# Experts' stage of a two-layer attention and expert network: loops written out, transposes one expert ahead, weights in two parts, finer waits at the tail

## The chip, the cores and the metric

One Trainium2 chip, one of its cores. The metric is the device time of one execution in microseconds; lower is better. The core has five engines that run side by side and meet at semaphores: TensorE (PE in the profile; PEld is its weight load), VectorE (DVE), ScalarE (ACT), GpSimd (POOL) and SyncE (SP), which issues most of the DMAs.

## What is computed

The whole reference is two layers, each an attention and a feed-forward part. The change touches only the last part, a mixture of experts over 2048 tokens of width 256:

```python
xt = x.reshape(T, d)                                    # T = 2048, d = 256
probs = softmax(xt @ Wg); eidx = argmax(probs); gate = probs[eidx]
pos = rank of the token among those of its expert
keep = pos < C                                          # C = 256, E = 8 experts
xd = rows of xt put at eidx * C + pos                   # (8, 256, 256)
h = silu(xd @ W1[e]) * (xd @ W3[e]); oe = h @ W2[e]     # hidden width 352
out = oe[eidx * C + pos] * gate * keep
shared = silu(xt @ sw1) * (xt @ sw3) @ sw2
x = x + out + shared
```

## The kernel before

`phase_moe` cuts its work into 16 pieces of 256 tokens. Eight are pieces of the shared network (0 to 7) and eight are the experts' own (0 to 7). TensorE runs them in this order: shared 0 to 5 (`HEAD` is 6), experts 0 to 7, shared 6 and 7 (`TAILS`). A piece has two parts. `hidden` (L2323) multiplies by the two upper weights, in three column blocks f = 0, 1, 2 (128, 128 and 96 wide), each block in its own PSUM bank `psH[f]`; every float32 matmul of the code is two instructions, so a block is 8 and a piece's `hidden` is 24. For every block ScalarE makes silu (`silu`, L2405), VectorE multiplies (`gated`, L2441, tile `g`). `down` (L2333) multiplies `g` by the lower weights, 12 instructions, into `psY[0]` and `psY[1]`; VectorE then adds the result to `x` (`add_shared`, L2449) or scales it by the gate into `yo` (`weigh`, L2457), and GpSimd scatters `yo` to `routed_scr` in DRAM with two indirect DMAs per expert (L2307).

In a shared piece TensorE runs block 0 of the piece, then `down` of the piece before, then blocks 1 and 2. In an expert's piece (`own`) the order is: four transposes of the expert's rows `xd[:, e]` into `psH[3]` (L2363), `down` of the piece before, then all three blocks. ScalarE copies the transposed rows to `xt` (L2410, in its `own`) before the expert's silus.

The rows of an expert come about so: logits and ranks are made on TensorE and VectorE while shared 0 and 1 run. Then GpSimd scatters the 16 row tiles with one indirect DMA each (L2300) to `xd_scr`, and SP, after waiting for all of them, loads `xd` for each expert (L2264).

On TensorE, ScalarE and VectorE shared pieces 2 to 5 (on ScalarE 0 to 5) are a hardware loop (`Fori`), on ScalarE the experts too, on SP the weight loads of experts 2 to 7. The double-buffered weights are loaded by four DMAs (`load_ffn`, L2231 to L2234) on one semaphore, when `down` of the expert two before is done (`y_full`). At the end SP waits for the last scatter, loads `back` from `routed_scr` in quarters (L2276), VectorE adds the quarters to `x` (L2528), the first three after the last `gated` and the fourth after the last `add_shared`, and SP sends every quarter out (L2281).

Of the kernel before, what the change touches and what calls it, by code (L numbers as in the profile page):

```python
# [9 lines left out]
ALU = mybir.AluOpType  # L10
# [6 lines left out]
P = 128  # L17
# [6 lines left out]
NT = B * ST  # L24
# [2134 lines left out]
def phase_moe(nc, ctx, t, keep, x, rows, xT):  # L2159
# [4 lines left out]
    def sem(name):  # L2164
        return new_semaphore(nc, "m_" + name)
# [41 lines left out]

    in_c, in_s, in_z = sem("in_c"), sem("in_s"), sem("in_z")
    in_w = [sem(f"in_w{i}") for i in range(2)]
    in_xd = [sem(f"in_xd{e}") for e in range(E1)]  # L2210
    in_back = [sem(f"in_back{k}") for k in range(4)]
    emptied, named, gates_ready = sem("emptied"), sem("named"), sem("gates_ready")
# [14 lines left out]
    TAILS = [(HEAD + E1 + i, HEAD + i) for i in range(NS - HEAD)]  # L2227
    norm = Norm(nc, ctx, keep, x, xn, xT, "m_", psH)

    def load_ffn(sp, s, d1, d3, d2, a1, a3, a2):  # L2230
        sp.dma_start(d1[:], a1.rearrange("(c d) f -> d c f", d=P)).then_inc(s, 16)  # L2231
        sp.dma_start(d3[:], a3.rearrange("(c d) f -> d c f", d=P)).then_inc(s, 16)
        sp.dma_start(d2[:, 0:2, :], a2[0:256, :].rearrange("(c f) d -> f c d", f=P)).then_inc(s, 16)
        sp.dma_start(d2[0:96, 2, :], a2[256:352, :]).then_inc(s, 16)  # L2234

    with nc.Block() as block:
        @block.sync
        def _(sp):
            sp.dma_start(ident[:], t["ident"]).then_inc(in_c, 16)
            sp.dma_start(upper[:], t["upper"]).then_inc(in_c, 16)  # L2240
            sp.dma_start(rank[:], t["rank"]).then_inc(in_c, 16)
            sp.dma_start(ebase[:], t["ebase"]).then_inc(in_c, 16)
            sp.dma_start(token[:], t["token"]).then_inc(in_c, 16)
            sp.dma_start(wg[:], t["L1_ffn_Wg"].rearrange("(c d) e -> d c e", d=P)).then_inc(in_c, 16)
            load_ffn(sp, in_s, sw1, sw3, sw2, t["L1_ffn_sw1"], t["L1_ffn_sw3"], t["L1_ffn_sw2"])
            sp.wait_ge(emptied, 2)
            for k in range(4):
                sp.dma_start(t["xd_scr"].rearrange("(k p r) d -> k p (r d)", k=4, p=P)[k],
                             empty[:].rearrange("p r d -> p (r d)")).then_inc(in_z, 16)

            def weights(e, u):
                ap = [a[bass.ds(e, 1)].rearrange("o a b -> (o a) b")
                      for a in (t["L1_ffn_W1"], t["L1_ffn_W3"], t["L1_ffn_W2"])]
                load_ffn(sp, in_w[u], w1[u], w3[u], w2[u], *ap)

            weights(0, 0)
            weights(1, 1)
            sp.wait_ge(zeroed, 1)
            for k in range(4):
                sp.dma_start(t["routed_scr"].rearrange("(k p r) d -> k p (r d)", k=4, p=P)[k],  # L2260
                             zero[:]).then_inc(in_z, 16)
            sp.wait_ge(scattered, 16 * NT)
            for e in range(E1):
                sp.dma_start(xd[:, e], t["xd_scr"][e * CAP1:(e + 1) * CAP1, :].rearrange("(c p) d -> p c d", p=P)  # L2264
                             ).then_inc(in_xd[e], 16)
            with sp.Fori(0, E1 // 2 - 1) as j:
                for u in range(2):
                    e = 2 * j + u

                    sp.wait_ge(y_full, 2 * (HEAD + e) + 2)  # L2270
                    weights(e + 2, u)
            for u in range(2):
                sp.wait_ge(sent[u], 32 * (E1 // 2))
            for k in range(4):
                rows_k = slice(k * NT // 4, (k + 1) * NT // 4)
                sp.dma_start(back[:, rows_k, :],  # L2276
                             t["routed_scr"].rearrange("(j p) d -> p j d", p=P)[:, rows_k, :]).then_inc(in_back[k], 16)
            for k in range(4):
                rows_k = slice(k * NT // 4, (k + 1) * NT // 4)
                sp.wait_ge(x_final, k + 1)  # L2280
                sp.dma_start(t["out"].rearrange("b (s p) d -> p (b s) d", p=P)[:, rows_k, :],  # L2281
                             x[:, rows_k, :]).then_inc(out_sent, 16)
            for u in range(2):
                sp.wait_ge(in_w[u], 64 * (E1 // 2))
            sp.wait_ge(out_sent, 64)

        @block.gpsimd
        def _(pool):
# [25 lines left out]
        def _(pe):  # L2314
# [34 lines left out]
            def shared(n, i, last):  # L2349

                moving = (lambda c: xT[:, c, i * CAP1:(i + 1) * CAP1] if isinstance(i, int) else
                          xT[:, c, bass.ds(i * CAP1, CAP1)])
                hidden(n, sw1, sw3, moving, 0)
                if last is not None:
                    down(*last)
                hidden(n, sw1, sw3, moving, 1)

            def own(e, j, u, last):
                pe.wait_ge(in_xd[e], 16)
                pe.wait_ge(xt_done, e + 1)  # L2360
                for c in range(DK):
                    for r in range(2):
                        mm = pe.transpose(psH[3][:, c * 256 + r * P:c * 256 + (r + 1) * P],  # L2363
                                          xd[:, e, r, c * P:(c + 1) * P], ident[:])
                mm.then_inc(xt_full, 1)
                down(*last)
                pe.wait_ge(in_w[u], 64 * j + 64)
                pe.wait_ge(xt_done, e + 2)
                hidden(HEAD + e, w1[u], w3[u], lambda c: xt[u][:, c, :], 0)
                hidden(HEAD + e, w1[u], w3[u], lambda c: xt[u][:, c, :], 1)  # L2370

            shared(0, 0, None)
            shared(1, 1, (0, sw2, 0))
# [8 lines left out]
                               ohb[:, j:j + 1, :].broadcast_to([P, left, E1]),  # L2382
                               start=False, stop=True, skip_group_check=True)
            mm.then_inc(cum_full, 1)
            with pe.Fori(1, HEAD // 2) as j:
                for u in range(2):
                    n = 2 * j + u
                    shared(n, n, (n - 1, sw2, 1 - u))
            own(0, 0, 0, (HEAD - 1, sw2, 1))
            for e in range(1, E1):  # L2390
                own(e, e // 2, e % 2, (HEAD + e - 1, w2[(e - 1) % 2], (e - 1) % 2))
            last = (HEAD + E1 - 1, w2[1], 1)
            for n, i in TAILS:
                shared(n, i, last)
                last = (n, sw2, n % 2)
            down(*last)

        @block.scalar
        def _(act):
# [5 lines left out]
                    nc.scalar.activation(act_s[u][0:fw, f, :], psH[f][0:fw, 0:CAP1], ACT.Silu  # L2405
                                         ).then_inc(silu_done, 1)

            def own(e, u):
                act.wait_ge(xt_full, e + 1)
                nc.scalar.activation(xt[u][:].rearrange("p c s -> p (c s)"), psH[3][:],  # L2410
                                     ACT.Copy).then_inc(xt_done, 1)
                silu(HEAD + e, u)

            norm.scalar_root(act)
            norm.scalar_columns(act)
            act.wait_ge(l_done, 2)
            nc.scalar.activation(ex[:], ex[:], ACT.Exp).then_inc(ex_ready, 1)
            with act.Fori(0, HEAD // 2) as j:
                for u in range(2):
                    silu(2 * j + u, u)  # L2420
            act.sem_inc(xt_done, 1)
            with act.Fori(0, E1 // 2) as j:
                for u in range(2):
                    own(2 * j + u, u)
            for n, _ in TAILS:
                silu(n, n % 2)

# [1 line left out]
        def _(dve):  # L2429
# [14 lines left out]
            def add_shared(n, i):  # L2444

                for r in range(2):
                    dve.wait_ge(y_full, 2 * n + r + 1)
                    row = x[:, bass.ds(2 * i + r, 1), :].rearrange("p o d -> p (o d)")
                    nc.vector.tensor_tensor(row, row, psY[r][:, 0:D], ALU.add).then_inc(y_done, 1)  # L2449

            def weigh(e):

# [46 lines left out]
            link(nc.vector.tensor_scalar(keepm[:], keepm[:], -OUT_OF_RANGE, OUT_OF_RANGE, ALU.mult, ALU.add))  # L2499
            link(nc.vector.tensor_tensor(slot[:], slot[:], keepm[:], ALU.add))  # L2500
            nc.vector.tensor_copy(s_idx[:], slot[:]).then_inc(idx_ready, 1)
            with dve.Fori(1, HEAD // 2) as j:
                for u in range(2):
                    n = 2 * j + u
                    gated(n, u, (0,))
                    add_shared(n - 1, n - 1)
                    gated(n, u, (1, 2))
            add_shared(HEAD - 1, HEAD - 1)
            for e in range(E1):
                if e > 0:  # L2510
                    weigh(e - 1)
                gated(HEAD + e, e % 2)
            for k, (n, i) in enumerate(TAILS):
                gated(n, n % 2, (0,))
                if k == 0:
                    weigh(E1 - 1)
                else:
                    add_shared(n - 1, i - 1)
                gated(n, n % 2, (1, 2))

            dve.wait_ge(y_done, 2 * n + 2)
            for k in range(4):
                rows_k = slice(k * NT // 4, (k + 1) * NT // 4)
                if k == 3:
                    add_shared(n, i)
                    dve.wait_ge(y_done, 2 * n + 4)
                dve.wait_ge(in_back[k], 16)
                nc.vector.tensor_tensor(x[:, rows_k, :], x[:, rows_k, :], back[:, rows_k, :],  # L2528
                                        ALU.add).then_inc(x_final, 1)

# [164 lines left out]
```

## Time and profile before

| | us |
|---|---|
| median of 3 runs | 1718.06 (1713.58 to 1718.11) |
| the profiled execution's own time | 1718.32 |
| its span, first to last instruction | 1716.5 |
| mean granted TensorE clock | 0.97 |
| last stage's first instruction to the end of the span | 1534.6 to 1716.5 |

Engines' busy shares over the span are PE 95%, DVE 77%, ACT 59%, POOL 58%. The profile is of one execution, and times in the rows are microseconds from the start of its span. A row's bracket says how long the engine had been idle before and what released it.

### The profile page before, as it was taken

To read this page: it belongs to the slowest core of one execution; us is meant where nothing else is said; L and a number is where in the kernel's file an instruction comes from. 1 tells how busy PE (TensorE), PEld (TensorE's weight loads), DVE (VectorE), ACT (ScalarE), POOL (GpSimd) and SP (SyncE) were. 2 spreads that over 40 slices of the span, in tenths; PEclk is the share of its full clock that TensorE was granted. 3 is DMA by queue.
4 is the path that set the end of the run, shared out by engine and by line. 5 is a ranking of instruction groups with operands and counts; after the bars stand their busy time and mean duration, and the time that the engine had idled before them with its cause. 6 is when DMAs were issued, how large, how long until landed. Compare 5 with 4: busy or idle time off the path is not lost. (4 is left out here: it accounts for less than half of the span.)

```text
span 1716.5 us, 49117 instructions
## 1 busy us (share of the span) xinstructions
PE 1632.6 (95%) x16165; PEld 1311.5 (76%) x16165; DVE 1320.2 (77%) x3025; ACT 1018.0 (59%) x2039; POOL 991.8 (58%) x879
## 2 busy tenths in 40 slices
PE   5889999999999999999999999999999899969898
PEld 4678888888888888888888888887886455548676
DVE  6888888888888888888888888887884588873123
ACT  5876666666666666666666666665333466642111
POOL 5348777878878787778788787777000222211221
PEclk8599999999999999999999999999999999987999
DMA  9721121121121122122112116114820000013244
GB/s 254 245 69 44 52 72 47 46 79 43 41 82 42 43 71 58 39 62 63 47 54 70 43 47 152 41 49 121 178 58 1 13 14 13 12 64 133 84 156 141
DMA packets 183005, 126.16 MB, mean 73 GB/s; under 512 B 107434, under 2 KB 170200, under 8 KB 182576
## 3 DMA queue, kind: packets, MB, share of 16 engines
q1 hardware_dynamic: 181424, 121.60, 25.7%
q0 software_dynamic: 1536, 3.99, 0.6%
q8 instruction: 25, 0.41, 0.1%
q14 instruction: 20, 0.16, 0.0%
HBM read 82.04 MB, written 24.48 MB: 62 GB/s over the span
## 5 line engine op out<-in xcount | busy, mean ns | idle before, releaser
L1174 POOL TENSOR_TENSOR c_rest<-c_prob 128x1024 f16<-128x1024 f32 (+1 forms) x513 | 796.0, 1572 | 242.8 <-ACT c_prob L963 232.5
L963 ACT ACTIVATE c_prob<-c_psS,ln,c_exp_scale 128x1024 f32<-128x1024 f32 (+1 forms) x514 | 536.5, 1044 | 241.2 <-PE c_psS L799 236.0
L1068 DVE TENSOR_REDUCE c_mxp<-c_psM 128x1 f32<-128x400 f32 (+1 forms) x1040 | 588.4, 572 | 113.8 <-PE c_psM L783 97.0
L799 PE MATMUL c_psS<-c_q,c_kk 128*128 128x256 f16 (+1 forms) x3350 | 512.7, 272 | 0.2 <-issue 0.2
L817 PE MATMUL c_psV<-c_vb,c_prob 128*128 128x129 f16 (+1 forms) x3328 | 396.5, 222 | 0.7 <-ACT c_acc L1017 0.7
L799 PEld LDWEIGHTS c_psS<-c_q,c_kk 128*128 128x128 f16 (+1 forms) x3350 | 321.8, 99 | 85.7 <-issue 0.4
L820 PE MATMUL c_psV<-c_vb,c_rest 128*128 128x65 f16 (+1 forms) x3328 | 374.2, 193 | 0.0
L783 PE MATMUL c_psM<-c_kkm,c_q 128*128 128x400 f16 (+1 forms) x1040 | 346.1, 333 | 4.7 <-DVE c_mxp L1068 3.0
L820 PEld LDWEIGHTS c_psV<-c_vb,c_rest 128*128 128x128 f16 (+1 forms) x3328 | 301.4, 99 | 22.1
L817 PEld LDWEIGHTS c_psV<-c_vb,c_prob 128*128 128x128 bf16 (+1 forms) x3328 | 305.3, 97 | 15.3 <-ACT c_acc L1017 1.0
L745 PE MATMUL c_psQ<-c_xb,c_w2s 128*128 128x256 f16 x1188 | 164.1, 275 | 5.8 <-PEq L162 4.0
L2051 ACT ACTIVATE g_prob<-g_psS,g_bias 128x128 f32<-128x128 f32 (+1 forms) x264 | 106.6, 425 | 47.3 <-DVE g_bias L2092 47.3
L745 PEld LDWEIGHTS c_psQ<-c_xb,c_w2s 128*128 128x128 f16 x1188 | 102.8, 98 | 23.0 <-issue 6.9
L1844 POOL TENSOR_TENSOR km<-kT,g_hmask 128x1024 f32<-128x1024 f32 x18 | 34.1, 1915 | 136.3 <-PE g_psS L1957 136.3
L783 PEld LDWEIGHTS c_psM<-c_kkm,c_q 128*128 128x128 f16 x1040 | 101.7, 98 | 14.2 <-DVE c_mxp L1068 3.9
L770 PE MATMUL c_psQ<-c_roped,c_ms 128*128 128x256 f32 x396 | 101.5, 392 | 0.6 <-DVE c_roped L1052 0.6
L951 ACT ACTIVATE c_q<-c_psM 32x128 f16<-32x128 f16 x258 | 68.9, 267 | 49.2 <-PE c_psM L787 47.8
L2405 ACT ACTIVATE m_s<-m_psH 128x256 f32<-128x256 f32 (+1 forms) x48 | 18.3, 382 | 114.4 <-PE m_psH L2323 108.5
L939 ACT ACTIVATE c_q<-c_psQ 64x256 f16<-64x256 f32 x132 | 49.8, 378 | 50.3 <-PE c_psQ L770 48.7
L1239 POOL TENSOR_SCALAR xn_rows<-x_rows,f_n_agg,f_n_rstd 128x256 f32<-128x256 f32 x3 | 3.9, 1315 | 127.3 <-DVEq L1256 127.3
L2441 DVE TENSOR_TENSOR m_g<-m_s,m_psH 128x256 f32<-128x256 f32 (+1 forms) x48 | 20.2, 420 | 72.8 <-ACT m_s L2405 62.0
L770 PEld LDWEIGHTS c_psQ<-c_roped,c_ms 128*128 128x128 f32 x396 | 70.0, 190 | 7.6 <-DVE c_roped L1052 0.8
(301 smaller groups left out, 2266.0 us busy)
## 6 DMA issues: line engine op xcount, KB each, us to landing
c_w2s<-w_scr SPq DMA_DIRECT2D x66, 256.0 KB, 2.6
c_ms<-m_scr SPq DMA_DIRECT2D x67, 192.0 KB, 2.3
c_w2s<-w_scr SPq DMA_DIRECT2D x66, 128.0 KB, 2.0
acc_scr<-c_acc SPq DMA_DIRECT2D x129, 64.0 KB, 2.0
kv<-acc_scr SPq DMA_DIRECT2D x16, 512.0 KB, 6.6
m_w<-in_L_ffn_W SPq DMA_DIRECT2D x16, 352.0 KB, 4.2
c_vb<-V SPq DMA_DIRECT2D x27, 129.0 KB, 2.0
c_kk<-KK SPq DMA_DIRECT2D x27, 128.0 KB, 2.0
```

Source lines behind the costliest of these rows:

```text
L745: mm = pe.matmul(out, weights[:, w, c], xb[:, x, c, :], start=(c == 0 and i == 0), stop=(c == DK - 1 and i == 2))
L770: mm = pe.matmul(psQ[:, S:2 * S], ms[:, e, :], roped[:, e, :], start=(e == 0), stop=(e == 2))
L783: pe.matmul(psM[:, st, 0:w], q1[slot][:, st * P:(st + 1) * P], kkm[:, c0:c0 + w], start=True, stop=True).then_inc(mx_full, 1)
L799: mm = pe.matmul(psS[g % 2][0:r, i * S:(i + 1) * S], src[:, (lo + i) * P:(lo + i) * P + r], mov[slot][:, :], start=(one == 0 and i % 2 == ...
L817: pe.matmul(psV[:, st * W:(st + 1) * W], high[0:r, c0:c0 + P], vb[0:r, i, :], start=(i == 0 and st == 0), stop=False, skip_group_check=True)
L820: mm = pe.matmul(psV[:, st * W + DC:(st + 1) * W], rest[g][0:r, c0:c0 + P], vb[0:r, i, DC:W], start=False, stop=(i == LT - 1), skip_group_ ...
L939: nc.scalar.activation(q1[slot + u][rows, :], psQ[rows, S:2 * S], ACT.Copy).then_inc(qh_done, 1)
L951: last = nc.scalar.activation(q2[slot][0:2 * SHIFT_ROWS, st * P:(st + 1) * P], shiftT[st * 2 * SHIFT_ROWS:(st + 1) * 2 * SHIFT_ROWS, :], A ...
L963: nc.scalar.activation(prob[g][0:r, 0:w], psS[g % 2][0:r, 0:w], ACT.Exp, bias=keep["ln1024"][0:r, :], scale=exp_scale[slot][0:r, :]).then_ ...
L1068: nc.vector.tensor_reduce(mxp[:, st, c:c + 1], psM[:, st, 0:CHUNKS[c][1]], AX.X, ALU.max).then_inc(mx_done, 1)
L1174: nc.gpsimd.tensor_tensor(rest[g][0:r, 0:w], prob[g][0:r, 0:w], high[0:r, 0:w], ALU.subtract).then_inc(rest_done, 1)
L2051: ins = nc.scalar.activation(prob[k % 2][:, i * w:(i + 1) * w], psS[k % 2][:, i * w:(i + 1) * w], ACT.Exp, bias=bias[k % 2][:, i:i + 1], a ...
```

## The change

The loops of TensorE, ScalarE, VectorE and SP in this stage are written out. An expert's piece takes the order of a shared piece, block 0, `down` of the piece before, blocks 1 and 2, with the transposes of the next expert between `down` and block 1. The first expert's transposes stand in shared 5. The upper weights wait for `h_full` of the expert two before, the lower ones for its `y_full`, on semaphores of their own (`in_w`, `in_d`). At the tail, the last `down` runs block by block for both halves (`down_last`), the quarters of `back` are added earlier, and the last four row tiles leave in three DMAs.

```diff
+    in_d = [sem(f"in_d{i}") for i in range(2)]
...
-            with sp.Fori(0, E1 // 2 - 1) as j:
-                for u in range(2):
-                    e = 2 * j + u
-
-                    sp.wait_ge(y_full, 2 * (HEAD + e) + 2)
-                    weights(e + 2, u)
+            for e in range(2, E1):
+                sp.wait_ge(h_full, FTN * (HEAD + e - 2) + FTN)
+                up(e)
+                sp.wait_ge(y_full, 2 * (HEAD + e - 2) + 2)
+                lower(e)
...
-            for k in range(4):
-                rows_k = slice(k * NT // 4, (k + 1) * NT // 4)
-                sp.wait_ge(x_final, k + 1)
-                sp.dma_start(t["out"].rearrange("b (s p) d -> p (b s) d", p=P)[:, rows_k, :],
-                             x[:, rows_k, :]).then_inc(out_sent, 16)
+            for lo, hi in ((0, 4), (4, 8), (8, 12), (12, 14), (14, 15), (15, 16)):
+                sp.wait_ge(x_final, min(lo // 4 + 1, 4))
+                if lo >= NT - 2:
+                    sp.wait_ge(y_done, 2 * TAILS[-1][0] + 3 + lo - (NT - 2))
+                sp.dma_start(t["out"].rearrange("b (s p) d -> p (b s) d", p=P)[:, lo:hi, :],
+                             x[:, lo:hi, :]).then_inc(out_sent, 16)
...
                 hidden(n, sw1, sw3, moving, 0)
                 if last is not None:
+                    if n == HEAD + E1:
+                        pe.wait_ge(in_d[(E1 - 1) % 2], 32 * ((E1 - 1) // 2) + 32)
                     down(*last)
+                if n == HEAD - 1:
+                    transposes(0)
                 hidden(n, sw1, sw3, moving, 1)
...
-                down(*last)
-                pe.wait_ge(in_w[u], 64 * j + 64)
+
+            def own(e, last):
+                u = e % 2
+                pe.wait_ge(in_w[u], 32 * (e // 2) + 32)
                 pe.wait_ge(xt_done, e + 2)
                 hidden(HEAD + e, w1[u], w3[u], lambda c: xt[u][:, c, :], 0)
+                if e > 0:
+                    pe.wait_ge(in_d[1 - u], 32 * ((e - 1) // 2) + 32)
+                down(*last)
+                if e + 1 < E1:
+                    transposes(e + 1)
                 hidden(HEAD + e, w1[u], w3[u], lambda c: xt[u][:, c, :], 1)
+
+            def down_last(n, a2, u):
+                pe.wait_ge(y_done, 2 * n + 2)
+                for f, (_, fw) in enumerate(FT1):
+                    pe.wait_ge(g_done, FTN * n + 4 + f)
+                    for r in range(2):
+                        mm = pe.matmul(psY[r][:, 0:D], g[u][0:fw, f, r * P:(r + 1) * P], a2[0:fw, f, :],
+                                       start=(f == 0), stop=(f == FTN - 1))
+                        if f == FTN - 1:
+                            mm.then_inc(y_full, 1)
...
-            with pe.Fori(1, HEAD // 2) as j:
-                for u in range(2):
-                    n = 2 * j + u
-                    shared(n, n, (n - 1, sw2, 1 - u))
+            for n in range(2, HEAD):
+                shared(n, n, (n - 1, sw2, 1 - n % 2))
...
+            for n in range(HEAD + E1):
+                silu(n, n % 2, (0,))
+                if HEAD - 1 <= n < HEAD + E1 - 1:
+                    columns(n - HEAD + 1)
+                silu(n, n % 2, (1, 2))
...
+            def add_routed(k):
+                rows_k = slice(k * NT // 4, (k + 1) * NT // 4)
+                dve.wait_ge(in_back[k], 16)
+                nc.vector.tensor_tensor(x[:, rows_k, :], x[:, rows_k, :], back[:, rows_k, :],
+                                        ALU.add).then_inc(x_final, 1)
...
-                gated(n, n % 2, (1, 2))
-
-            dve.wait_ge(y_done, 2 * n + 2)
-            for k in range(4):
-                rows_k = slice(k * NT // 4, (k + 1) * NT // 4)
-                if k == 3:
-                    add_shared(n, i)
-                    dve.wait_ge(y_done, 2 * n + 4)
-                dve.wait_ge(in_back[k], 16)
-                nc.vector.tensor_tensor(x[:, rows_k, :], x[:, rows_k, :], back[:, rows_k, :],
-                                        ALU.add).then_inc(x_final, 1)
+                    dve.wait_ge(y_done, 2 * n + 2)
+                for f in (1, 2):
+                    if k == 1:
+                        add_routed(f - 1)
+                    gated(n, n % 2, (f,))
+            add_routed(2)
+            add_routed(3)
+            dve.wait_ge(x_final, 4)
+            add_shared(n, i)
```

## Rows read from the trace of the kernel before

**Rows 1.** The chain that ended last: start us, us, what.

```profile
1588.10 2.60 PE m_psY L2333 x12
1590.69 5.18 PE m_psH L2323 x24
1595.88 6.90 issue
1602.78 5.15 PE m_psY L2333 x12
```

**Rows 2.** Timeline, 1590 to 1604: start us, us, engine, line, op.

```profile
1590.53 5.34 PE L2323 MATMUL m_psH<-xT_rows,m_sw 128*128 x24
1596.85 0.38 ACT L2405 ACTIVATE m_s<-m_psH 128x256 f32<-128x256 f32 x1 [8.33 <-PE m_psH L2323]
1601.81 0.38 ACT L2405 ACTIVATE m_s<-m_psH 96x256 f32<-96x256 f32 x1 [4.58 <-remote]
...
1603.57 4.22 SPq L2264 DMA_DIRECT2D m_xd<-xd_scr  x8
```

**Rows 3.** The scatter's line L2300: durations ns min/median/max, first and last start.

```profile
L2300 POOL DMA_INDIRECT xd_scr<-xn_rows,m_s_idx x16: 972/972/1307, 1581.8 to 1601.3; - x16
```

**Rows 4.** A stretch: us, busy PE PEld DVE ACT POOL, PEclk, DMA share, GB/s.

```profile
1603.00:1619.00 16.00, 16.00 (x64) 13.07 (x64) 3.78 (x9) 2.40 (x6) 0.00 (x0) 0.86 0.44 133
```

**Rows 5.** Timeline of one expert's piece, 1631 to 1646.

```profile
1631.76 5.34 PE L2323 MATMUL m_psH<-m_xt,m_w 128*128 128x256 f32 x24
...
1636.94 0.60 PE L2363 MATMUL m_psH<-m_ident,m_xd 128*128 128x128 f32 x4
...
1637.55 0.42 DVE L2441 TENSOR_TENSOR m_g<-m_s,m_psH 96x256 f32<-96x256 f32 x1 [1.30 <-ACT m_s L2405]
...
1638.02 2.86 PE L2333 MATMUL m_psY<-m_w,m_g 128*128 128x256 f32 x12 [0.48 <-DVE m_g L2441]
...
1640.72 5.34 PE L2323 MATMUL m_psH<-m_xt,m_w 128*128 128x256 f32 x24
```

**Rows 6.** Timeline of the tail, 1702 to 1716.

```profile
1702.84 3.62 PE L2323 MATMUL m_psH<-xT_rows,m_sw 128*128 128x256 f32 x16
1703.04 0.42 DVE L2449 TENSOR_TENSOR x_rows<-x_rows,m_psY 128x256 f32<-128x256 f32 x1 [0.88 <-PE m_psY L2333]
...
1705.18 0.42 DVE L2441 TENSOR_TENSOR m_g<-m_s,m_psH 128x256 f32<-128x256 f32 x1 [1.72 <-ACT m_s L2405]
...
1706.90 0.42 DVE L2441 TENSOR_TENSOR m_g<-m_s,m_psH 96x256 f32<-96x256 f32 x1 [1.30 <-ACT m_s L2405]
1707.24 3.48 DVE L2528 TENSOR_TENSOR x_rows<-x_rows,m_back 128x1024 f32<-128x1024 f32 x3
...
1707.38 2.86 PE L2333 MATMUL m_psY<-m_sw,m_g 128*128 128x256 f32 x12 [0.92 <-DVE m_g L2441]
1708.48 4.57 SPq L2281 DMA_DIRECT2D out_dram<-x_rows  x4
1710.65 0.74 DVE L2449 TENSOR_TENSOR x_rows<-x_rows,m_psY 128x256 f32<-128x256 f32 x2
1711.42 1.23 DVE L2528 TENSOR_TENSOR x_rows<-x_rows,m_back 128x1024 f32<-128x1024 f32 x1
```

**Rows 7.** The loads of the experts' rows, L2264.

```profile
DMA to landing us min/median/max: 2.7/5.1/5.8
```

**Rows 8.** The loads of the experts' results, L2276, issued from 1699.0 to 1700.6.

```profile
DMA to landing us min/median/max: 3.8/5.4/6.8
```

**Rows 9.** The stores of the output, L2281.

```profile
DMA to landing us min/median/max: 3.0/3.4/3.8
```

**Rows 10.** The first of an expert's four weight DMAs, L2231.

```profile
DMA to landing us min/median/max: 3.2/3.4/6.5
```

**Rows 11.** TensorE's loop branches, lines L893 (attention of layer 0) and L2385.

```profile
L893 PEldq COMPARE_BRANCH  x32: 76/208/252, 140.8 to 1188.5; - x32
...
L2385 PEldq COMPARE_BRANCH  x2: 76/146/217, 1590.2 to 1615.2; - x2
```

More of the change, by code:

```diff
@@ L2228, in phase_moe, with load_up, load_down @@
     norm = Norm(nc, ctx, keep, x, xn, xT, "m_", psH)
-    def load_ffn(sp, s, d1, d3, d2, a1, a3, a2):
+    def load_up(sp, s, d1, d3, a1, a3):
         sp.dma_start(d1[:], a1.rearrange("(c d) f -> d c f", d=P)).then_inc(s, 16)
         sp.dma_start(d3[:], a3.rearrange("(c d) f -> d c f", d=P)).then_inc(s, 16)
+    def load_down(sp, s, d2, a2):
         sp.dma_start(d2[:, 0:2, :], a2[0:256, :].rearrange("(c f) d -> f c d", f=P)).then_inc(s, 16)
@@ L2244, in _ @@
             sp.dma_start(wg[:], t["L1_ffn_Wg"].rearrange("(c d) e -> d c e", d=P)).then_inc(in_c, 16)
-            load_ffn(sp, in_s, sw1, sw3, sw2, t["L1_ffn_sw1"], t["L1_ffn_sw3"], t["L1_ffn_sw2"])
+            load_up(sp, in_s, sw1, sw3, t["L1_ffn_sw1"], t["L1_ffn_sw3"])
+            load_down(sp, in_s, sw2, t["L1_ffn_sw2"])
             sp.wait_ge(emptied, 2)
@@ L2249, in _, with up, lower @@
                              empty[:].rearrange("p r d -> p (r d)")).then_inc(in_z, 16)
[L2251 to L2257, printed above, removed]
+            def up(e):
+                load_up(sp, in_w[e % 2], w1[e % 2], w3[e % 2], t["L1_ffn_W1"][e], t["L1_ffn_W3"][e])
+            def lower(e):
+                load_down(sp, in_d[e % 2], w2[e % 2], t["L1_ffn_W2"][e])
+            for e in range(2):
+                up(e)
+                lower(e)
             sp.wait_ge(zeroed, 1)
@@ L2265, in _ @@
                              ).then_inc(in_xd[e], 16)
-            with sp.Fori(0, E1 // 2 - 1) as j:
-                for u in range(2):
-                    e = 2 * j + u
-                    sp.wait_ge(y_full, 2 * (HEAD + e) + 2)
-                    weights(e + 2, u)
+            for e in range(2, E1):
+                sp.wait_ge(h_full, FTN * (HEAD + e - 2) + FTN)
+                up(e)
+                sp.wait_ge(y_full, 2 * (HEAD + e - 2) + 2)
+                lower(e)
             for u in range(2):
@@ L2277, in _ @@
                              t["routed_scr"].rearrange("(j p) d -> p j d", p=P)[:, rows_k, :]).then_inc(in_back[k], 16)
-            for k in range(4):
-                rows_k = slice(k * NT // 4, (k + 1) * NT // 4)
-                sp.wait_ge(x_final, k + 1)
-                sp.dma_start(t["out"].rearrange("b (s p) d -> p (b s) d", p=P)[:, rows_k, :],
-                             x[:, rows_k, :]).then_inc(out_sent, 16)
+            for lo, hi in ((0, 4), (4, 8), (8, 12), (12, 14), (14, 15), (15, 16)):
[4 more added lines that the diff above has]
+                             x[:, lo:hi, :]).then_inc(out_sent, 16)
             for u in range(2):
-                sp.wait_ge(in_w[u], 64 * (E1 // 2))
-            sp.wait_ge(out_sent, 64)
+                sp.wait_ge(in_w[u], 32 * (E1 // 2))
+                sp.wait_ge(in_d[u], 32 * (E1 // 2))
+            sp.wait_ge(out_sent, 96)
         @block.gpsimd
@@ L2354, in shared, with transposes @@
                 if last is not None:
+                    if n == HEAD + E1:
+                        pe.wait_ge(in_d[(E1 - 1) % 2], 32 * ((E1 - 1) // 2) + 32)
                     down(*last)
+                if n == HEAD - 1:
+                    transposes(0)
                 hidden(n, sw1, sw3, moving, 1)
-            def own(e, j, u, last):
+            def transposes(e):
                 pe.wait_ge(in_xd[e], 16)
@@ L2384, in _ @@
             mm.then_inc(cum_full, 1)
-            with pe.Fori(1, HEAD // 2) as j:
-                for u in range(2):
-                    n = 2 * j + u
-                    shared(n, n, (n - 1, sw2, 1 - u))
-            own(0, 0, 0, (HEAD - 1, sw2, 1))
+            for n in range(2, HEAD):
+                shared(n, n, (n - 1, sw2, 1 - n % 2))
+            own(0, (HEAD - 1, sw2, 1))
             for e in range(1, E1):
-                own(e, e // 2, e % 2, (HEAD + e - 1, w2[(e - 1) % 2], (e - 1) % 2))
+                own(e, (HEAD + e - 1, w2[(e - 1) % 2], (e - 1) % 2))
             last = (HEAD + E1 - 1, w2[1], 1)
@@ L2395, in _ @@
                 last = (n, sw2, n % 2)
-            down(*last)
+            down_last(*last)
         @block.scalar
@@ L2406, in silu, with columns @@
                                          ).then_inc(silu_done, 1)
-            def own(e, u):
+            def columns(e):
                 act.wait_ge(xt_full, e + 1)
-                nc.scalar.activation(xt[u][:].rearrange("p c s -> p (c s)"), psH[3][:],
+                if e >= 2:
+                    act.wait_ge(h_full, FTN * (HEAD + e - 2) + FTN)
+                nc.scalar.activation(xt[e % 2][:].rearrange("p c s -> p (c s)"), psH[3][:],
                                      ACT.Copy).then_inc(xt_done, 1)
-                silu(HEAD + e, u)
             norm.scalar_root(act)
@@ L2417, in _ @@
             nc.scalar.activation(ex[:], ex[:], ACT.Exp).then_inc(ex_ready, 1)
-            with act.Fori(0, HEAD // 2) as j:
-                for u in range(2):
-                    silu(2 * j + u, u)
             act.sem_inc(xt_done, 1)
-            with act.Fori(0, E1 // 2) as j:
-                for u in range(2):
-                    own(2 * j + u, u)
+            for n in range(HEAD + E1):
[3 more added lines that the diff above has]
+                silu(n, n % 2, (1, 2))
             for n, _ in TAILS:
@@ L2501, in _ @@
             nc.vector.tensor_copy(s_idx[:], slot[:]).then_inc(idx_ready, 1)
[L2502 to L2508, printed above, removed]
+            for n in range(2, HEAD):
+                gated(n, n % 2, (0,))
+                add_shared(n - 1, n - 1)
+                gated(n, n % 2, (1, 2))
             for e in range(E1):
+                gated(HEAD + e, e % 2, (0,))
                 if e > 0:
                     weigh(e - 1)
-                gated(HEAD + e, e % 2)
+                else:
+                    add_shared(HEAD - 1, HEAD - 1)
+                gated(HEAD + e, e % 2, (1, 2))
             for k, (n, i) in enumerate(TAILS):
```

## The prediction

> **What bounds the kernel now.** I read the chain that ended last first, because a share of busy time says nothing about one stage. In the stage that changes it lies almost wholly on TensorE. Two kinds of step recur: 24 instructions of `hidden` in 5.18 us and 12 of `down` in 2.60 us [rows 1], which is 0.216 us an instruction for both. A shared piece is therefore 36 x 0.216 = 7.78 us, with no gap. Everything that the chain has beyond 7.78 us a piece is what a reorder can win. There are three such places.
>
> First, a hole. After 24 instructions that end at 1595.88 the chain has 6.90 us of "issue", then a `down` of 5.15 us in place of 2.60 [rows 1]. The timeline shows what happened: TensorE has its 24 instructions down as 5.34 us from 1590.53, but ScalarE, which is to start silu on the first 8 of them at about 1592.4, starts at 1596.85, and on the next 8, due near 1594.2, at 1601.81 [rows 2]. TensorE's signals came late, or its work did; the profile doesn't say which. `down` then needed the late `g`. The granted clock of the stretch from 1603 to 1619 is 0.86 [rows 4], where 1.00 is full, after an idle TensorE; the 5.15 us are the instructions at half of the clock (1.2 in place of 2.4 GHz). The hole costs 6.90 + (5.15 - 2.60) = 9.45 us.
>
> Second, the experts. From the 24 instructions at 1631.76 to the next at 1640.72 are 8.96 us [rows 5], eight times over. Over 7.78 us that is 1.18 us: the transposes, and a `down` that stands behind silu and `gated` of the last block: it starts at 1638.02, while the block's last matmul was followed by the transposes at 1636.94.
>
> Third, the tail. TensorE's last 16 instructions of `hidden` end at 1702.84 + 3.62 = 1706.46; `down` starts at 1707.38, VectorE adds three quarters until 1710.7, adds `psY`, and adds the last quarter until 1712.65; the span ends at 1716.5 [rows 6].
>
> **The change, part by part.** *Experts' order.* `down` moves behind block 0 of the next piece, which is 8 x 0.216 = 1.73 us and covers the 1638.02 - 1636.94 = 1.08 us in which silu and `gated` of the last block were awaited. The transposes move behind `down`. Their cost in the stream isn't 4 x 0.273: the group of four is 0.60 us with the last one's own tail in it [rows 5], so the next instruction can follow after between (0.60 - 0.27) x 4/3 = 0.44 and 0.60 us. I take 0.50, since the weight load that follows may show a little. The piece becomes 7.78 + 0.50 = 8.28, in place of 8.96: 0.68 us won, between 0.58 and 0.74, for eight experts 5.4 us (4.6 to 5.9). New waits: block 0 of an expert needs `xt`, whose copy (0.60 us) has all 16 instructions of blocks 1 and 2 (3.46 us) for cover; block 1's silu stands behind this copy on ScalarE, but is due 1.7 us after the transposes end, so it isn't late. VectorE has `weigh` (0.48 us each) between block 0 and block 1, where a shared piece has its two adds without harm.
>
> *Weights in two parts.* The upper ones are issued when `hidden` of the expert two before ends and are needed one piece later, 8.28 us; the second of the two DMAs goes some 0.5 us after the first, and they land after 3.2 to 6.5 us [rows 10], so 7.0 us at worst. The lower ones go out 4.3 us later and are needed nearly two pieces later. On SP the upper weights of the next expert stand behind the wait for `y_full`, which comes first anyway. Zero, and if the cover were gone, every microsecond counts six times.
>
> *Loops written out.* TensorE's two branches here take 76 and 217 ns on a sequencer that runs ahead of the engine, like 32 others in an earlier stage [rows 11]; those of the other engines, which idle most of this stage, lie in that idle time. Zero for these by themselves; what they have to do with the hole is a rival below.
>
> *First transposes in shared 5.* They need `xd[0]`: first issue 1603.57 [rows 2], fastest landing 2.7 us [rows 7], 1606.3. With the hole as it is, TensorE comes there near 1607.93 + 5.18 + 2.60 = 1615.7. Zero.
>
> *Tail.* `down_last` needs only block 2 of `g` late: 8 of its 12 instructions run from 1706.3 on, block 2's `g` is there at 1707.32, and the last instruction starts 12 x 0.216 later than the first, so both halves are ready at 1706.31 + 11 x 0.216 + 0.38 = 1709.07. VectorE: the quarters of `back` land between 1699.05 + 3.8 = 1702.9 and 1700.6 + 6.8 = 1707.4 [rows 8]. The first add (1.21 us, a pace of 1.14) fits between the add that ends at 1703.46 and `gated` at 1705.18; the second between 1705.60 and 1706.90, with 0.1 us to spare [rows 6]. Then 1707.24 to 1708.4, the fourth to 1709.6, then two adds of 0.37 to 1710.4, where before the last add ended at 1712.65: 2.25 us. The last store was of 512 KB; stores of this size take 3.0 to 3.8 us [rows 9]. The last one is now 128 KB, behind 256 and 128 KB, with some 0.45 us between issues. The bytes that are still to go when the third quarter leaves at 1708.48 are 512 + 512 KB. Before, the last issue was at 1708.48 + 4.57 - 0.37 = 1712.68 [rows 6] and landed about 3.4 us later, at 1716.1. With issues 1.14 us apart the stores' landing times grew by some 0.4 us from one to the next (3.0, 3.4, 3.8), so a quarter flows in 1.5 us: 1708.48 + 3.0 + 1.5 = 1713.0 for all. I take 3.0 us (2.2 if the last lands as late as a full one, 3.5 if the small ones are quick).
>
> **Sum.** Against the profiled execution's own 1718.3 (0.26 above the median of the runs): 1718.3 - 5.4 - 3.0 = 1709.9 us, hole unchanged. With both bounds 1708.9 to 1711.5.
>
> **The rivals.** *A: the hole goes away.* It appears at 1590.5, where TensorE's loop branches back (1590.2, [rows 11]), and the loop is written out. Then 9.4 us more are won: 1718.3 - 8.4 - 9.4 = 1700.5. TensorE would come to the first transposes at 1595.88 + 2.60 + 7.78 = 1606.3, just when `xd[0]` lands, so nothing is given back. Against it: 32 branches of the same length in an earlier stage, with no such hole in the chain. What this place has and they haven't are GpSimd's 16 indirect DMAs, from 1581.8 to 1602.2 [rows 3]: the hole ends with them, and the change leaves them alone. For it: the scatter had run for 9 us without harm when the branch came, and the fastest run of three, 1713.58, is 4.5 below the others, so the hole may be of varying length.
> The Trainium skill (Runtime: NRT & Kernel Launch, Instruction fetch mechanics) says that a taken branch whose target is outside the fetched window stalls on a fetch from memory; by it alone the hole would be the branch's and the time 1700.5. The trace doesn't bear this out well: TensorE's instructions after the branch are down as started at once [rows 2].
>
> *B: half of the hole.* The late signals depend on what TensorE has queued; if the hole lasts some 4.7 us the time is near 1705.
>
> *C: no change that can be measured.* A new wait eats the gains: above all `gated` of blocks 1 and 2 of the last piece now stands behind `back`. If the quarters land 2 us later than [rows 8] (the stores now share the DMAs with them), the tail's 3.0 us are lost; with transposes that cost 1.18 us as they did, the experts' too: 1714 to 1718.
>
> *D: slower, by one mechanism: late upper weights.* With pieces of 8.28 us they are covered as long as they land within 7.8 us of the first issue. Beyond that each of six experts waits. To lose the 8.4 us and 5 more, they must be 13.4 / 6 = 2.2 us late each, landing after 10 us. The slowest here took 6.5 [rows 10]. At 10.5 us: 1718.3 - 8.4 + 16 = 1726.
>
> **How the numbers follow.** Hole unchanged 0.52; A 0.28; B 0.07; C 0.08; D 0.05. The likeliest gives 1709.9, its own range is 1708.5 to 1712. The range over all reaches to A, below it by A's own bounds, and leaves out C and D: 1699.5 to 1713.0. A measurement of this kernel can't tell less than 0.3%, 5.2 us, from no change. Faster by more: the first three, 0.87. Within: 0.08. Slower: 0.05.
>
> **What would show it.** The chain after: experts' pieces at 8.2 to 8.4 us, with no wait of `down` for `gated`; ScalarE's idle between silus of one piece as in a shared one; no TensorE wait for `in_w`. The hole: silus of shared 3 late by 4 to 8 us, or not. The tail: last VectorE add 4 us after the last `hidden`, and 7 us from the last `hidden` to the end of the span, in place of 10. I am wrong if the experts' pieces stay near 9 us, if VectorE waits for `back` ahead of the last `gated`, or if the hole grows or goes.

## The result, and the profile after

| | us |
|---|---|
| before, median of 4 runs | 1718.07 (1713.58 to 1718.11) |
| changed, median of 4 runs | 1704.51 (1702.37 to 1706.27) |
| ratio | 0.9926, 95% interval 0.9908 to 0.9943 |
| profiled execution, own time and span | 1702.37, 1700.5 |

The change is 0.7% faster: 13.6 us by the medians, 16.0 between the two profiled spans. The chain that ended last in the changed kernel (start us, us, what) shows the hole and two experts' pieces:

```profile
1590.23 5.18 PE m_psH L2330 x24
1595.41 1.15 issue
1596.56 2.86 PE m_psY L2340 x12
1599.42 3.46 PE m_psH L2330 x16
1602.88 0.72 issue
1603.59 1.99 PE m_psH L2330 x8
1605.59 0.02 issue
1605.61 2.86 PE m_psY L2340 x12
1608.47 0.44 PE m_psH L2374 x4
1608.91 5.18 PE m_psH L2330 x24
1614.10 2.60 PE m_psY L2340 x12
1616.69 0.44 PE m_psH L2374 x4
1617.13 5.18 PE m_psH L2330 x24
```

A hole is meant here as in the prediction: a gap in TensorE's chain that no recorded work explains. Where [rows 1] have 6.90 us of "issue" and a `down` at half of the clock, there are now 1.15 and 0.72 us, and `down` takes 2.86 at a granted clock of 1.00. The experts' pieces follow each other without a gap: from 1608.91 to 1617.13 are 8.22 us, where [rows 5] have 8.96. ScalarE's rows in the hole (timeline, idle before and its releaser in brackets) say that TensorE's signals are still late:

```profile
1592.81 0.38 ACT L2431 ACTIVATE m_s<-m_psH 128x256 f32<-128x256 f32 x1 [4.76 <-PE m_psH L2330]
...
1595.68 0.38 ACT L2431 ACTIVATE m_s<-m_psH 96x256 f32<-96x256 f32 x1 [2.48 <-PE m_psH L2330]
...
1602.70 0.39 ACT L2431 ACTIVATE m_s<-m_psH 128x256 f32<-128x256 f32 x1 [6.64 <-remote]
```

In an undisturbed piece these idle times are 3.94, 1.34 and 1.35 us. The same three silus in a later profile of the kernel before, which has no hole (its 24 instructions of `hidden` start at 1598.62):

```profile
1600.55 0.38 ACT L2405 ACTIVATE m_s<-m_psH 128x256 f32<-128x256 f32 x1 [3.94 <-PE m_psH L2323]
...
1602.27 0.38 ACT L2405 ACTIVATE m_s<-m_psH 96x256 f32<-96x256 f32 x1 [1.34 <-PE m_psH L2323]
...
1604.00 0.38 ACT L2405 ACTIVATE m_s<-m_psH 128x256 f32<-128x256 f32 x1 [1.35 <-PE m_psH L2323]
```

They start 1.93, 3.65 and 5.38 us after the first of the 24. In the changed kernel, whose 24 start at 1590.07, they are 0.8, 2.0 and 7.3 us later than that; in [rows 2], with the third silu at 1604.73, 4.4, 7.6 and 8.8 us. So the first two signals were late by much less and the third by nearly as much, and it is the second that `down` waits for. The last late silu starts 2.5 us after the last scatter's row ends in the first kernel's profile (1602.2) and 0.9 us after it in this one (1601.8); from there on the signals are on time.

The tail (timeline; the rows that answer to [rows 6]):

```profile
1689.60 3.62 PE L2330 MATMUL m_psH<-xT_rows,m_sw 128*128 128x256 f32 x16
...
1690.25 1.22 DVE L2480 TENSOR_TENSOR x_rows<-x_rows,m_back 128x1024 f32<-128x1024 f32 x1
...
1691.94 0.42 DVE L2467 TENSOR_TENSOR m_g<-m_s,m_psH 128x256 f32<-128x256 f32 x1 [0.47 <-ACT m_s L2431]
1692.28 1.22 DVE L2480 TENSOR_TENSOR x_rows<-x_rows,m_back 128x1024 f32<-128x1024 f32 x1
...
1693.05 2.75 PE L2395 MATMUL m_psY<-m_sw,m_g 128*128 128x256 f32 x12
...
1693.66 0.42 DVE L2467 TENSOR_TENSOR m_g<-m_s,m_psH 96x256 f32<-96x256 f32 x1 [0.17 <-ACT m_s L2431]
1694.00 2.35 DVE L2480 TENSOR_TENSOR x_rows<-x_rows,m_back 128x1024 f32<-128x1024 f32 x2
1696.39 0.75 DVE L2475 TENSOR_TENSOR x_rows<-x_rows,m_psY 128x256 f32<-128x256 f32 x2
```

The first two quarters are added while TensorE still works on blocks 1 and 2 (the second ends 0.3 us after them); neither delays `gated`, whose bracket names ScalarE. The last `down` (L2395) follows `hidden` without the 0.92 us of [rows 6]. VectorE ends at 1697.14, 3.9 us after the last `hidden`; the span ends at 1700.5, 7.3 us after it, where it was 10.0.

Cut at the same events, the two profiles give:

| stretch | before | after | won |
|---|---|---|---|
| span's start to the last rank matmuls (PE m_psR x15) | 1578.00 | 1577.54 | 0.5 |
| to the end of shared 5's `hidden` | 41.18 | 34.83 | 6.35 |
| to the end of expert 7's `hidden` | 71.73 | 65.30 | 6.4 |
| to the end of the span | 25.59 | 22.83 | 2.8 |

The 0.5 of the first row is what two differences leave, neither of them the change's work: the stage's first matmul comes 1.6 us later in the changed kernel's profile (1545.49, before 1543.88), and from there to the rank matmuls it takes 2.1 us less (32.05, before 34.12; the last section has more on this).

### The profile page after: what moved, and what is told of

Same layout as the page of the kernel before. It is cut to its first block and busy times, and to the rows that moved or that the text cites. A ratio compares the mean times of both kernels' runs of the same rounds, so it can differ in the third digit from the quotient of the medians.

```text
span 1700.5 us, 48945 instructions
## 1 busy us (share of the span) xinstructions
PE 1627.4 (96%) x16165; PEld 1308.5 (77%) x16165; DVE 1320.6 (78%) x3025; ACT 1015.7 (60%) x2037; POOL 993.7 (58%) x879
## 5 line engine op out<-in xcount | busy, mean ns | idle before, releaser
L2092 DVE TENSOR_REDUCE g_bias<-g_psS 128x4 f32<-128x1024 f32 (+1 forms) x49 | 59.9, 1223 | 13.6 <-PE g_psS L1957 11.2
```

## The experiments

They ran on three chips (5, 12 and 1), each beside runs of the kernel before on the same chip. The number of the first comparison's chip isn't known. That matters: on these three the kernel before took 1706.5 to 1707.6 us in the median, and none of its 64 reference runs more than 1709.58; in the first comparison its median was 1718.07, and the fastest run 1713.58.

**Controls.** The kernel before, and the changed one twice, without an edit.

> The kernel before, unchanged, as a control. 'Execution' (the hole belongs to some chips or executions, not to the code): a profile without the hole, 1708, as the four runs just made show none of any length; or with it, 1718. 'Code' (it is in this kernel whatever the chip): a hole of 9 us in this profile.

> The changed kernel, unchanged, as a control beside the kernel before on the same chip. If the hole belongs to the execution: no hole, experts' pieces 8.22 us, tail as measured, and the gain over before is that of order and tail alone, 5.9 + 2.8 = 8.7 us, 0.995. If the loops mattered as well, more than 12 us, under 0.993.

> The changed kernel again, unchanged, to see whether the hole in TensorE's signals comes back. Without a hole: 1698 to 1700 and 8 us under before; with it, 2 to 7 us more, and the kernel before near 1718 on the same chip.

Measured: the kernel before as a control 1706.8 us, 0.9998 (0.9988 to 1.0008) of its like. Changed kernel 1698.77, ratio 0.9954 (0.9940 to 0.9967), and on a third chip 1700.29, 0.9962 (0.9950 to 0.9975). The chain of the kernel before, at the place of [rows 1]:

```profile
1591.01 5.18 PE m_psH L2323 x24
1596.19 2.60 PE m_psY L2333 x12
1598.78 5.18 PE m_psH L2323 x24
1603.96 2.60 PE m_psY L2333 x12
```

The code is that of [rows 1], the loop branches and the 16 indirect DMAs are there, and there is no hole. So it isn't the code's alone. Against a kernel before without it, the change wins 7.9 us (1 - 0.9954 of 1707) and 6.5 us (1 - 0.9962), not 13.6. The interval of the second, 4.3 to 8.5 us, just holds the 8 that were expected.

The changed kernel's chain on that chip shows what stands where the hole was:

```profile
1596.23 2.38 DMA xd_scr<-xn_rows,m_s_idx
1598.62 0.02 issue
1598.63 2.79 DMA m_xd<-xd_scr
1601.43 0.04 issue
1601.47 0.66 PE m_psH L2374 x4
1602.13 5.18 PE m_psH L2330 x24
```

The chain now runs through GpSimd's scatter and the load of `xd[0]` to the first transposes, which waited 0.28 us for it (0.2 on the third chip). The scatter has no slack left.

**Loops written out, alone, and the loops put back.**

```diff
-            with pe.Fori(1, HEAD // 2) as j:
-                for u in range(2):
-                    n = 2 * j + u
-                    shared(n, n, (n - 1, sw2, 1 - u))
+            for n in range(2, HEAD):
+                shared(n, n, (n - 1, sw2, 1 - n % 2))
```

The first run makes this edit, and its like on ScalarE and VectorE, to the kernel before; the second undoes it in the changed kernel, with `transposes(0)` and `columns(0)` behind shared 5. Neither touches the other loops of the change, ScalarE's over the experts and SP's over their weights.

> The kernel before with the loops of shared pieces 2 to 5 written out on TensorE, ScalarE and VectorE; experts and tail as they were. Theory 'branch' (the hole of 9.45 us comes from the loops): the hole shrinks as it did in the changed kernel, to about 2.7 us, so 6.8 us are won, 1711. Theory 'scatter' (the hole belongs to the 16 indirect DMAs, its length is chance or depends on the experts' order): the hole stays near 9.4 us, 1718.

> The changed kernel with the loops of shared pieces 2 to 5 put back on TensorE, ScalarE and VectorE; the first expert's transposes and their copy stand after shared 5. Experts' order, two-part weights and tail as changed. 'Branch': the hole is back at 9 us and the time 1704.5 + 6.8 = 1711. 'Scatter, and chance': 1704 to 1706, or the spread of before.

Measured: 1707.99 us, ratio 1.0003 (0.9994 to 1.0013), and 1699.35, 0.9945 (0.9926 to 0.9964). No hole in either profile, nor in the kernel before on this chip by its 1707.6 us. So the runs don't tell whether the loops change a hole; they show that without one these loops cost nothing that can be measured, and that the changed kernel with them is as fast as without. Its chain shows what the first expert costs when its transposes aren't ahead:

```profile
1609.00 0.63 PE m_psH L2372 x4
1609.63 0.73 issue
1610.36 1.97 PE m_psH L2330 x8
```

**One indirect DMA of 16.** The kernel before, edited so. It leaves out the scatter of 15 of the 16 row tiles, so most rows never reach their expert and the output is wrong; the work on all engines but GpSimd is the same.

```diff
-            sp.wait_ge(scattered, 16 * NT)
+            sp.wait_ge(scattered, 16)
...
-            for j in range(NT):
+            for j in range(1):
                 nc.gpsimd.indirect_dma_start(
```

> The kernel before with one of the 16 indirect DMAs that fill xd_scr left out for all but the first row tile (15 of 16 row tiles of the experts' rows are left out), loops as they were. 'Scatter': no hole, silus of shared 3 follow their matmuls within 0.2 us; 9.4 us are won at the hole and the first transposes no longer wait for anything: 1708 to 1709. 'Branch': the hole of 9 us stays, 1718.

Measured: 1707.99 us, 1.0007 (0.9997 to 1.0017). There was no hole to take away on this chip, so it decides nothing on the cause. It does show that in the kernel before the other 15 scatters cost nothing where there is no hole.

**The tail alone.** `down_last`, the earlier adds of `back` and the six stores, as in the diff of the change, on the kernel before.

> The kernel before with the tail's part of the change alone (last down block by block, earlier adds of back, last four row tiles in three stores). From the last hidden to the end of the span 7.2 us in place of 10.0: 2.8 us faster, 1715.3, hole as before. Rival: the tail's gain depends on the other parts, then under 1 us.

Measured: 1705.49 us, 0.9986 (0.9977 to 0.9996), which is 2.4 us of 1707.6 (0.7 to 3.9).

**The order alone.** The changed kernel with the loops of shared 2 to 5 and the old tail.

```diff
-            down_last(*last)
+            down(*last)
...
-            for lo, hi in ((0, 4), (4, 8), (8, 12), (12, 14), (14, 15), (15, 16)):
+            for lo, hi in ((0, 4), (4, 8), (8, 12), (12, 16)):
```

> The kernel before with the experts' order, transposes one expert ahead and two-part weights, but the loops of shared 2 to 5 and the old tail. Experts' pieces 8.22 us in place of 8.96: 5.9 us won, less 0.7 for a first expert that waits for its copy: 5.2 us, 0.997. Rival (order and tail not additive): under 4.

Measured: 1703.56 us, 0.9978 (0.9966 to 0.9990), 3.8 us of 1707.1 (1.7 to 5.8); its pieces take 8.21 us in the chain. That is below the 5.2 expected and by the number alone in the rival's range, though the interval holds both. The profiles say where most of it went: from the end of shared 5's `hidden` to that of expert 7's this run takes 67.21 us and the kernel before 71.70, 4.5 won. The first expert, whose transposes aren't ahead, costs 1.5 us more than in the changed kernel (0.32 until they start, then 0.63 + 0.73 + 0.24 in place of 0.44), where 0.7 was expected. Order and tail together, 6.2 us, lie within the errors of the 7.9 and of the 9.4 (0.9945) of the run with kept loops.

**Upper weights late.** The changed kernel, all four DMAs of an expert behind `y_full`:

```diff
-                sp.wait_ge(h_full, FTN * (HEAD + e - 2) + FTN)
-                up(e)
                 sp.wait_ge(y_full, 2 * (HEAD + e - 2) + 2)
+                up(e)
                 lower(e)
```

> The changed kernel with all four weight DMAs of an expert waiting for y_full of the expert two before, as the kernel before had it. The time left for the upper weights falls from 8.2 to 3.9 us, and two of them with 0.5 us between issues land some 4.1 to 5 us after the first issue. If the two-part load matters: TensorE waits 0.3 to 1.3 us in each of six pieces, 2 to 8 us slower than the changed kernel. Rival (weights hidden anyway): no wait, same time.

Measured: 1705.28 us, 0.9990 (0.9980 to 1.0001), against 0.9954 of the changed kernel on the same chip: 6.1 us of its gain are gone. The chain goes through the DMA six times:

```profile
1628.07 1.99 PE m_psH L2329 x8
1630.06 2.61 PE m_psY L2339 x12
1632.67 0.02 issue
1632.68 0.37 SPq L2232
1633.05 0.04 issue
1633.10 4.28 DMA m_w<-in_L_ffn_W
1637.38 0.04 issue
1637.42 1.99 PE m_psH L2329 x8
```

From block 0 to block 0 are 9.35 us in place of 8.22 here, and between 8.95 and 9.69 in the six pieces. From the end of shared 5's `hidden` to that of expert 7's the run takes 72.13 us, the changed kernel on the same chip 65.29, so the six lose 6.8 us. The loads are issued when `down` ends and have 3.9 us; they take 0.4 + 4.3. TensorE's row has the wait of 0.87; the rest of the 1.13 us is that block 0 takes 1.99 us in the chain after a wait, and 1.73 without one:

```profile
1637.42 1.99 PE L2329 MATMUL m_psH<-m_xt,m_w 128*128 128x256 f32 x8 [0.87 <-DMA m_w<-in_L_ffn_W]
```

**Transposes not ahead.** The changed kernel, `down` still behind block 0, but each expert's transposes at the head of its own piece and the copy before its silus:

```diff
             def own(e, last):
                 u = e % 2
+                transposes(e)
                 pe.wait_ge(in_w[u], 32 * (e // 2) + 32)
...
-                if e + 1 < E1:
-                    transposes(e + 1)
...
-                silu(n, n % 2, (0,))
-                if HEAD - 1 <= n < HEAD + E1 - 1:
-                    columns(n - HEAD + 1)
-                silu(n, n % 2, (1, 2))
+                if n >= HEAD:
+                    columns(n - HEAD)
+                silu(n, n % 2)
```

> The changed kernel with each expert's transposes at the head of its own piece, as before, but down still behind block 0. Theory 'both moves are needed': block 0 now waits for the copy of the transposes, as the first expert's did in the run with kept loops (0.63 + 0.73 + 0.24 us in place of 0.44), so a piece takes 7.78 + 1.60 = 9.38 us, more than the 8.96 of before, and the eight cost 9.3 us over the changed kernel. Rival 'moving down is what wins': pieces of 8.3 to 8.5 us, within 2 us of the changed kernel.

Measured: 1707.68 us, 1.0006 (0.9996 to 1.0015), against 0.9962 of the changed kernel on the same chip: 7.5 us of its gain are gone (eight pieces by 0.96 are 7.7).

```profile
1627.96 0.44 PE m_psH L2372 x4
1628.39 0.73 issue
1629.13 1.97 PE m_psH L2330 x8
1631.09 2.60 PE m_psY L2340 x12
1633.69 3.45 PE m_psH L2330 x16
1637.14 0.44 PE m_psH L2372 x4
```

A piece takes 9.18 us, 0.22 more than before the change: the copy of the transposed rows, which `down` used to cover, is bare. Expected were 9.38 us a piece, and 9.3 us in all; the transposes cost 0.44, not 0.63, since they follow matmuls.

## Why the prediction was right, and where it was off

*Experts' order: right, a little small.* 8.22 us a piece where 8.28 were forecast, because four transposes cost 0.44 us, the lower bound; 0.74 us for each of eight is 5.9, where 5.4 stood. The run with transposes not ahead shows that moving `down` doesn't help without the other move: with it alone a piece is 0.22 us longer than before. Transposes ahead with `down` in its old place were not tried.

*Weights in two parts: right, and not free.* Zero for the split as made, no wait in the chain. The run with late upper weights shows what the cover is worth, and that rival D had the right mechanism: beyond the time that is left, each of six experts waits.

*Loops: zero, shown* for those of shared 2 to 5 by 1.0003 (0.9994 to 1.0013); the experts' loops on ScalarE and SP weren't undone by themselves. The rule of the Trainium skill on taken branches (Runtime: NRT & Kernel Launch, Instruction fetch mechanics) doesn't explain the hole: the kernel before has the same branch, 225 ns at 1590.5, in a profile without one. Nor is the branch needed for a hole of 2.68 us, since the changed kernel has none in this stage. So rival A's branch is neither enough for a hole nor needed for one, though it may still have lengthened the first.

*Tail: 3.0 forecast, 2.8 in the profiles, 2.4 (0.7 to 3.9) alone.* The adds fell where they were put. VectorE's last add 3.9 us after `hidden` was right; from there to the end of the span are 3.4 us, where the forecast had 1713.0 for the last landing, 2.6 us behind the last add, and so some 3.0 to the end of the span; before they were 3.85 (1716.5 - 1712.65).

*The hole: the term of the sum that was off.* "Hole unchanged" was the likeliest case, and it failed. In the profiles it shrank from 9.47 us (41.18, less the 31.71 that the stretch takes in the control without it) to 2.68 (34.83 - 31.71 - 0.44 for the first transposes). That is rival B with another length (6.8 us shorter, not 4.7), and it is what put the median, 1704.5, 5.4 us below the 1709.9. That the time came out inside the range is therefore in part luck: the range was drawn wide to reach rival A, and half of the distance to the kernel before comes from a term that was forecast to stay. I had taken the hole for a part of the kernel, with one cause in its code. The controls show that it is no fixed part: the same kernel had it in the first comparison and not on chip 12, and its times on chips 5 and 1 leave no room for it. Without it the change brings 6.5 to 7.9 us, near the 8.4 of the sum. So of the 13.6 us of the first comparison some 6.5 to 8 are the change's and the rest, 6 to 7, those of a hole that was shorter in the runs of the changed kernel (6.8 us shorter in the one profile of each). Whether the change shortened it, or the executions differ by chance, stays open: no profile after the first two showed it, so the runs that were to tell branch and scatter apart could not. What is shown is that branch and scatters together aren't enough, as the control has both and no hole. That the late signals end near the last scatter in both profiles speaks for the scatters' having a part in it, but no run shows that they are needed.

*What it gave up.* The first transposes now wait 0.2 to 0.3 us for the scatter and the load of `xd[0]`, where they had 3.5 us of slack in the control before: its last scatter starts at 1601.6, scatter and load take 5.24 us (1596.23 to 1601.47 above), and its first transposes run at 1610.35. I had forecast this for the case without a hole, at 1606.3 against 1606.3.

## What to carry to other kernels

Fill the wait of a short chain (silu, multiply) with a block of the next piece's matmuls, but look at what stood behind the moved instruction: here the copy of the transposes lost its cover and had to go one piece ahead, and the weights, loaded as before, would have had 3.9 us in place of a whole piece of 9.0, and had to be split. Undo each part alone before you call it a help or a nuisance. And when a profile has one gap that its kind of code shows nowhere else, profile the same kernel once more, on another chip and at another time, before you give that gap to the change.

## What the runs showed of the hardware

TensorE's signals can be late by several microseconds while its matmuls are down as started at their usual pace: in the first kernel's profile a silu started at 1596.85 after a matmul group that ends near 1592.4 [rows 2], in a stretch with 16 indirect DMAs. This was seen in the two profiles of the first comparison and in none of ten on chips 5, 12 and 1, nine of which have the 16 DMAs. Whether it belongs to that chip or to that time isn't known. In the first profile TensorE has no matmul from 1595.9 to 1602.8, and its granted clock is 1.00 until 1600.5 and 0.50 from 1601.

The stage's entry costs one of two amounts. The 64 logit instructions take 9.7 to 10.0 us in seven of the twelve profiles and 12.2 in five (9.72, 9.96 and 9.73 in the changed kernel, 12.17 and 12.15 in the kernel before, 9.76 with its loops out, 12.18 with its tail changed), though no edit touches them. One stretch of the kernel before and of the changed one (us, busy PE, PEld, DVE, ACT and POOL, then the granted clock, DMA share and GB/s):

```profile
1551.50:1560.00 8.50, 8.50 (x48) 8.50 (x48) 0.00 (x0) 0.76 (x1) 0.00 (x0) 0.58 0.86 329
```

```profile
1551.50:1560.00 8.50, 7.86 (x56) 7.86 (x57) 0.00 (x0) 1.87 (x3) 0.00 (x0) 0.80 1.05 379
```

TensorE idles 10.3 us before this stage, for the layer norm, with the clock at its lower level (0.50). In both profiles the clock rises between 1549 and 1550, during the stage's transposes, and falls back to 0.50 while the logit matmuls, 8 columns wide, still run without a pause: near 1553 in the kernel before (0.50 from 1553 to 1556, where the changed kernel has 1.00), near 1556.7 in the changed one (0.50 from 1557 to 1560). It rises again between 1566 and 1567 in both. So what differs between the profiles is how many of the logit matmuls still get the full clock. From the stage's first matmul to the first `down` the two profiles take 28.0 and 25.9 us.

No kernel was profiled with both amounts, so the profiles alone leave open whether the amount belongs to the execution or to the kernel, and in the second case 2 us would be won or lost by an edit that has nothing to do with them. The times speak for the execution: the kernel before with its loops out has 9.76 us in its profile and is no faster than the kernel before, which has 12.15 (1.0003), and late weights and transposes not ahead, both with 12.2 us, lose 6.1 and 7.5 us against the changed kernel, where the experts' stretch alone explains 6.8 and 7.7. The start of the stage, from 1541.2 to 1545.5 in the twelve profiles, differs by more.
